# Issuing the load of xs from ScalarE's queue, behind that of xg, in the second stage of a graph-GRU kernel

## The chip, the cores and the metric

The kernel runs on one core of one Trainium2 chip. The metric is the device time of one launch in microseconds. Three runs of the kernel before gave 2310.07, 2310.32 and 2313.84 us; their median is 2310.32 us.

## The reference

For each of 2048 samples x is a matrix of 50 nodes by 32 features. Two maskers (T = 2) make an adjacency matrix each out of the sample, a gated cell mixes neighbours with it, and then come a batch norm, a layer norm and an attention pooling:

```python
adj = relu(einsum('bn,tnm->btm', x.reshape(b, 1600), masker_param) + masker_bias).reshape(b, 2, 50, 50)
adj = adj / (adj.sum(-1, keepdims=True) + 1e-6)
h = broadcast(x, (b, 2, 50, 32))
m = einsum('btnm,btmd->btnd', adj, h @ weight)
r, z, ng = split(m @ w_ih.T + b_ih + h @ w_hh.T + b_hh, 3)
h = (1 - sigmoid(z)) * tanh(sigmoid(r) * ng) + sigmoid(z) * h
# batch norm over b, layer norm over (t, n, d), softmax of scores over n, weighted sum over n
```

## The kernel before

All three stages run on one core, one after the other. Samples come in 16 tiles of 128.

**Stage 1** (up to about 1466 us of the profile) computes the adjacency in split float32 products and stores it, transposed, in the DRAM tensor `adjT`. **Stage 2** (about 1468 to 2080 us) is the gated cell. **Stage 3** does the norms and the pooling. The change touches stage 2 alone.

In stage 2 a tile is worked off in 8 rounds (`ROUNDS`), called q = 0 to 7 here; two tiles, r = 0 and 1, make one iteration of a hardware loop (16 steps, s = 8r + q; iterations 1 to 6 are the loop, 0 and 7 stand outside of it). The buffers `adj_sb`, `xs_sb` and `xg_sb` are double, one half for each r. `xs` holds x by node, padded with zeros (tensor `xz`), and `xg` holds the same x by feature.

- **TensorE** (`turn`, line 720): in step s it first aggregates the next step, `aggregate(s + 1)` (matmuls of `xs` and `adj`, line 674, into a PSUM bank), then does `gates(s)`: the matmuls of the r and z gates (line 699), four transposes of an earlier tile's result (`turn_chunks`, line 716), and the matmuls of the n gate (line 705). `gates` waits for `m_ready`, the low half of the aggregate, which VectorE writes (line 570). At s = 6 and 14 it waits until `adj_loaded[r]` has counted the three transfers of a tile: two halves of the adjacency and `xs`, 16 each, so 48 (lines 682 to 685).
- **ScalarE** (`turn`, line 507), in order: `m_hi` of the next step (line 490), in four of the eight rounds a part of `xg_hi` (line 486), the sigmoid of r in two halves (line 520), the sigmoid of z in two halves (line 525, after `h_ready` of the step before), the copy of four transposes to `hC` (line 498), the tanh (line 530, after `n_in`), the store of that `hC` (line 505), and at q = 0 of a tile the load of `xg` for the next tile (line 477).
- **VectorE** (`turn`, line 616), in order: `m_lo` of the next step (line 570), `n_in` (line 580), the statistics of `hC` (line 603, after `hC_ready`), the three operations that end the cell (lines 590, 593 and 595, after the tanh), and in four of the eight rounds a transpose of `hG` into `hT` (line 614).
- **SyncE** only loads: once `ax_done` says that tile t has been aggregated it issues the three transfers of tile t + 2 into the buffers that are free by this, in the order adjacency half 0, adjacency half 1, `xs`.

An adjacency half is moved in runs of 256 bytes (64 float32), 5000 of them; `xs` is moved in 100 rows of 16 KB.

Of the kernel before, what the change touches and what calls it, by code (L numbers as in the profile page):

```python
# [58 lines left out]
ROUNDS = 32 // QB  # L59
# [18 lines left out]
def wait(eng, sem, value):  # L78

    if not (isinstance(value, int) and value <= 0):  # L80
        eng.wait_ge(sem, value)
# [297 lines left out]
def stage2(nc, psum, ins, adjT, hF, stats):  # L379


    with ExitStack() as ctx:
# [3 lines left out]
        xs = sb("xs_sb", [2 * N, 2, SH, 2 * D])  # L386
# [23 lines left out]
        adj_loaded = [sem("adj_loaded0"), sem("adj_loaded1")]  # L410
        xg_loaded = [sem("xg_loaded0"), sem("xg_loaded1")]
        xg_hi_ready, xg_ready = sem("xg_hi_ready"), sem("xg_ready")
        ax_done, m_hi_ready, m_ready = sem("ax_done"), sem("m_hi_ready"), sem("m_ready")
# [11 lines left out]
        def rz_bank(pair):  # L425

            return psum[:, (2 + pair) * BANK:(2 + pair) * BANK + RC]
# [8 lines left out]
        @block.sync  # L436
        def _(sp):
            def load_adj(tile, r):
                for half in range(2):
                    sp.dma_start(adj[N * half:N * half + N, r], adjT[tile, :, SH * half:SH * half + SH].rearrange("(c m) s -> m c s", m=N)  # L440
                                 ).then_inc(adj_loaded[r], 16)
                sp.dma_start(xs[:, r], ins["xz"][tile]).then_inc(adj_loaded[r], 16)

            def load_xg(tile, r):
                sp.dma_start(xg[:, r], ins["xg"][tile]).then_inc(xg_loaded[r], 16)

            def iteration(it, more):
                for r in range(2):
                    tile = it * 2 + r
                    if more:  # L450
                        sp.wait_ge(ax_done, (tile + 1) * ROUNDS)
                        load_adj(tile + 2, r)

            for dst, src in ((wT4, "wT4"), (wih, "wihT"), (whh4, "whhT4"), (biases, "biases")):
                sp.dma_start(dst[:], ins[src]).then_inc(consts_loaded, 16)
            load_xg(0, 0)
            load_adj(0, 0)
            sp.dma_start(ident[:], ins["ident"]).then_inc(ident_loaded, 16)
            load_xg(1, 1)
            load_adj(1, 1)  # L460
            iteration(0, True)
            with sp.Fori(1, TILES // 2 - 1) as it:
                iteration(it, True)
            iteration(TILES // 2 - 1, False)
            for n in range(len(batches)):
                sp.wait_ge(hC_stored[n], 16 * TILES)

        @block.scalar
        def _(act):
            act.wait_ge(blocks_ready, 1)  # L470
            nc.scalar.copy(wd_hi[:], wd[:]).then_inc(wd_hi_ready, 1)
            act.wait_ge(bias_ready, 1)

            def load_xg(tile, r):

                act.wait_ge(h_ready, (tile - 1) * ROUNDS)
                nc.scalar.dma_start(xg[:, r], ins["xg"][tile]).then_inc(xg_loaded[r], 16)

            def x_hi(it, r, k):

                if k == 0:
                    act.wait_ge(xg_loaded[r], (it + 1) * 16)

                    wait(act, gates_done, it * S if r else it * S - ROUNDS)
                g = slice(k * XG, (k + 1) * XG)
                nc.scalar.copy(xg_hi[:, r, g], xg[:, r, g]).then_inc(xg_hi_ready, 1)  # L486

            def m_halves(it, s):
                act.wait_ge(ax_done, it * S + s + 1)
                nc.scalar.copy(m_hi[:, s % 2], ax_bank(s)).then_inc(m_hi_ready, 1)  # L490

            def evacuate(tile, n):

                act.wait_ge(turned, tile * len(batches) + n + 1)
                wait(act, hC_stored[n], 16 * tile)
                wait(act, bn_done, (tile - 1) * len(batches) + n + 1)
                c0, c1 = batches[n]
                nc.scalar.copy(hC[:, c0:c1, :].rearrange("p c b -> p (c b)"),  # L498
                               turn_bank[:, 0:(c1 - c0) * P]).then_inc(hC_ready, 1)

            def store(tile, n):

                act.wait_ge(hC_ready, tile * len(batches) + n + 1)
                c0, c1 = batches[n]
                nc.scalar.dma_start(hF[tile, :, c0:c1, :], hC[:, c0:c1, :]).then_inc(hC_stored[n], 16)

            def turn(it, more):
                for s in range(S):
                    r, q = divmod(s, ROUNDS)
                    if s + 1 < S or more:  # L510
                        wait(act, gates_done, it * S + s)
                        m_halves(it + (s + 1) // S, (s + 1) % S)
                    k = s % ROUNDS - (ROUNDS - XPARTS)
                    if 0 <= k < XPARTS and (s < ROUNDS or more):
                        x_hi(it + s // ROUNDS, 1 - s // ROUNDS, k)
                    act.wait_ge(rz_done, it * S + s + 1)
                    wait(act, n_in_ready, it * S + s)
                    for pair in range(2):
                        half = slice(SH * pair, SH * pair + SH)
                        last = nc.scalar.activation(r_gate[half], rz_bank(pair)[half], ACT.Sigmoid, bias=bias[half, R_G:R_G + 1])  # L520
                    last.then_inc(r_ready, 1)
                    wait(act, h_ready, it * S + s)
                    for pair in range(2):
                        half, other = slice(SH * pair, SH * pair + SH), slice(SH - SH * pair, 2 * SH - SH * pair)
                        last = nc.scalar.activation(z_bank[half], rz_bank(pair)[other], ACT.Sigmoid, bias=bias[other, Z_G:Z_G + 1])  # L525
                    last.then_inc(z_ready, 1)
                    if q and (r or not (isinstance(it, int) and it == 0)):
                        evacuate(it * 2 + r - 1, q - 1)
                    act.wait_ge(n_in_ready, it * S + s + 1)
                    nc.scalar.activation(n_bank(s), n_in[:, s % 2], ACT.Tanh).then_inc(n_ready, 1)  # L530
                    if q and (r or not (isinstance(it, int) and it == 0)):
                        store(it * 2 + r - 1, q - 1)
                    if q == 0 and (r and more or not r and not (isinstance(it, int) and it == 0)):
                        load_xg(it * 2 + r + 1, 1 - r)

            for k in range(XPARTS):
                x_hi(0, 0, k)
            m_halves(0, 0)
            turn(0, True)
            with act.Fori(1, TILES // 2 - 1) as it:  # L540
                turn(it, True)
            turn(TILES // 2 - 1, False)
            for n in range(len(batches)):
                evacuate(TILES - 1, n)
                store(TILES - 1, n)
# [810 lines left out]
```

## Time and profile before

| | us |
|---|---|
| median of three runs | 2310.32 (2310.07 to 2313.84) |
| the profiled execution's own time | 2318.24 |
| its span, first to last instruction | 2316.5 |
| ScalarE busy over the span | 962.2 (42%) |
| VectorE busy over the span | 1091.0 (47%) |
| TensorE busy over the span | 2198.9 (95%) |

Shares over the span mix three stages. Between 1700 and 1900 us, inside stage 2, TensorE is busy 199.98 of 200 us, VectorE 172.58 and ScalarE 177.36. The end of a matmul is modelled in the profile, so TensorE's share says that it has work queued, and the idle time before its weight loads (the engine name PEld) tells more about its waits. The queues from which transfers are issued are named SPq (SyncE) and ACTq (ScalarE); the time of a row there is that of the issue, not of the transfer.

### The profile page before, as it was taken

The numbers are of one execution on the slowest core, as the hardware profiler recorded it, in microseconds if no ns is written. First come the engines' busy times: TensorE is split into PE (matmuls) and PEld (weight loads), VectorE is DVE, ScalarE is ACT, GpSimd is POOL, SyncE is SP. The second block draws the span as 40 slices with busy tenths as digits, with TensorE's granted clock in tenths as the row PEclk, the third lists the DMA queues.
The fourth block names the chain that finished last, engine by engine and source line by source line (L and its number), as shares of the span: only waits on it lengthen the run. The fifth ranks groups of instructions, "written<-read, shape, count | busy, mean of one in ns | idle before, by whom it ended". The sixth has DMA issues, their size and how long they took to land. (4 is left out here: it accounts for less than half of the span.)

```text
span 2316.5 us, 34741 instructions
## 1 busy us (share of the span) xinstructions
PE 2198.9 (95%) x12302; PEld 1737.8 (75%) x12302; DVE 1091.0 (47%) x2177; ACT 962.2 (42%) x1637; POOL 136.2 (6%) x124
## 2 busy tenths in 40 slices
PE   8999999999999999999999999299999999975888
PEld 7888888888888888888888888277777777752333
DVE  4433233332345223333233332178888888873656
ACT  4322122221234212222122221088888988865551
POOL 0000000000000000000000000011101111104340
PEclk9999999999999999999999999699999999986899
DMA  6421222212234222221222211577777677619440
GB/s 208 151 75 44 88 91 90 74 45 88 92 128 143 64 90 90 91 69 50 89 90 91 72 48 27 124 171 184 186 201 181 188 199 181 181 65 261 122 119 5
DMA packets 341744, 264.06 MB, mean 114 GB/s; under 512 B 169334, under 2 KB 302998, under 8 KB 339990
## 3 DMA queue, kind: packets, MB, share of 16 engines
q1 hardware_dynamic: 323546, 225.69, 34.5%
q10 hardware_dynamic: 18144, 37.69, 5.0%
q8 instruction: 29, 0.48, 0.1%
q14 instruction: 25, 0.20, 0.0%
HBM read 195.65 MB, written 67.70 MB: 114 GB/s over the span
## 5 line engine op out<-in xcount | busy, mean ns | idle before, releaser
L340 PE MATMUL psum<-w_hi,x_lo 128*128 128x500 f32 x2080 | 823.0, 396 | 8.6 <-DVE w_lo L216 8.6
L340 PE MATMUL psum<-w_lo,x_hi 128*128 128x500 f32 (+1 forms) x2080 | 811.0, 390 | 0.0
L340 PE MATMUL psum<-w_hi,x_hi 128*128 128x500 f32 x1920 | 745.1, 388 | 0.0
L276 DVE TENSOR_REDUCE rows<-u 128x10 f32<-128x500 f32 x160 | 107.7, 673 | 893.5 <-ACT u L229 892.8
L340 PEld LDWEIGHTS psum<-w_hi,x_lo 128*128 128x128 f32 x2080 | 392.1, 188 | 84.4 <-issue 7.9
L340 PEld LDWEIGHTS psum<-w_lo,x_hi 128*128 128x128 f32 (+1 forms) x2080 | 392.5, 189 | 73.2
L340 PEld LDWEIGHTS psum<-w_hi,x_hi 128*128 128x128 f32 x1920 | 361.7, 188 | 72.9
L235 ACT COPY at<-psum 125x512 f32<-125x512 f32 x160 | 93.8, 586 | 677.4 <-PE psum L321 677.4
L229 ACT ACTIVATE u<-psum 128x500 f32<-128x500 f32 x160 | 94.1, 588 | 342.4 <-PE psum L340 342.3
L674 PE MATMUL psum<-adj_sb,xs_sb 100*64 100x100 f32 x2048 | 200.6, 350 | 30.1 <-DMA xs_sb<-xz 30.1
L674 PEld LDWEIGHTS psum<-adj_sb,xs_sb 100*64 100x64 f32 x2048 | 144.4, 149 | 73.9 <-issue 63.7
L652 POOL TENSOR_TENSOR xg_lo<-xg_sb,xg_hi 128x400 fp32r<-128x400 f32 x64 | 67.1, 1049 | 1961.4 <-ACT xg_hi L486 1961.4
L520 ACT ACTIVATE r_gate<-psum,bias 64x400 f32<-64x400 f32 x256 | 151.2, 591 | 18.3 <-PE psum L699 15.8
L216 DVE TENSOR_TENSOR w_lo<-w_raw,w_hi 128x1000 fp32r<-128x1000 f32 x120 | 144.1, 1201 | 23.6 <-ACT w_hi L210 17.4
L210 ACT CAST w_hi<-w_raw 128x1000 fp32r<-128x1000 f32 (+1 forms) x140 | 135.6, 969 | 46.3 <-PE psum L340 45.0
L525 ACT ACTIVATE psum<-psum,bias 64x400 f32<-64x400 f32 x256 | 142.3, 556 | 12.7 <-DVE hG L595 6.9
L284 DVE TENSOR_TENSOR an<-u,rows 128x500 f32<-128x500 f32 x160 | 108.8, 680 | 6.9
L603 DVE BATCH_NORM_STATS2 stats<-hC 128x128 f32 (+1 forms) x400 | 88.7, 282 | 49.3 <-ACT hC L498 48.9
L321 PEld LDWEIGHTS psum<-ident_sb,an 128*125 128x125 f32 x640 | 94.1, 186 | 17.8 <-DVE an L284 3.2
L321 PE MATMUL psum<-ident_sb,an 128*125 128x128 f32 x640 | 96.0, 272 | 4.0 <-DVE an L284 4.0
L1013 DVE SCALAR_TENSOR_TENSOR pr<-h,nmu_sb,psum 128x512 f32<-128x512 f32 x100 | 70.5, 743 | 47.0 <-PE psum L1221 24.6
L570 DVE TENSOR_TENSOR m_lo<-psum,m_hi 128x400 fp32r<-128x400 f32 x128 | 70.6, 552 | 28.6 <-ACT m_hi L490 28.6
(160 smaller groups left out, 2284.8 us busy)
## 6 DMA issues: line engine op xcount, KB each, us to landing
w_raw<-W SPq DMA_DIRECT2D x140, 500.0 KB, 7.9
adjT<-at SPq DMA_DIRECT2D x160, 250.0 KB
adj_sb<-adjT SPq DMA_DIRECT2D x32, 1250.0 KB
xs_sb<-xz SPq DMA_DIRECT2D x16, 1600.0 KB
hF<-hC ACTq DMA_DIRECT2D x96, 256.0 KB, 6.7
h<-hF SPq DMA_DIRECT2D x64, 256.0 KB, 4.5
xg_sb<-xg ACTq DMA_DIRECT2D x14, 800.0 KB, 8.0
h<-hF SPq DMA_DIRECT2D x48, 192.0 KB, 3.7
```

The source lines that it names most:

```text
L210: nc.scalar.copy(w_hi[:, k0:k1, :], w_raw[:, k0:k1, :]).then_inc(w_hi_ready, 1)
L216: nc.vector.tensor_tensor(w_lo[:, k0:k1, :], w_raw[:, k0:k1, :], w_hi[:, k0:k1, :].bitcast(fp32), ALU.subtract).then_inc(w_ready, 1)
L229: nc.scalar.activation(u[:, c2].rearrange("p n m -> p (n m)"), mm_out(c2), ACT.Relu).then_inc(u_ready, 1)
L235: nc.scalar.copy(at[:, c2].rearrange("p k b -> p (k b)"), tr_out(c2)).then_inc(at_ready, 1)
L276: nc.vector.tensor_reduce(rows[:, 0], u[:, c2], AX.X, ALU.add).then_inc(dve_step, 1)
L284: nc.vector.tensor_tensor(an[:, c2], u[:, c2], rows[:, 2].unsqueeze(2).to_broadcast([P, GN, N]), ALU.mult).then_inc(an_ready, 1)
L321: last = nc.tensor.transpose(tr_out(c2)[:, k * P:(k + 1) * P], flat[:, k * RK:(k + 1) * RK], ident[:, :])
L340: last = nc.tensor.matmul(mm_out(w % 2), a[0:r, k, cols], b[0:r, k, :], start=k == 0 and n == 0, stop=k == KF and n == 1)
L520: last = nc.scalar.activation(r_gate[half], rz_bank(pair)[half], ACT.Sigmoid, bias=bias[half, R_G:R_G + 1])
L525: last = nc.scalar.activation(z_bank[half], rz_bank(pair)[other], ACT.Sigmoid, bias=bias[other, Z_G:Z_G + 1])
L603: last = nc.vector.bn_stats(stats[:, bass.ds(tile, 1), c, :].rearrange("p i v -> p (i v)"), hC[:, c, :])
L674: last = nc.tensor.matmul(out_[SH * i:SH * i + SH, :, gi], xs[:, r, b, :], adj[:, r, :, b], start=True, stop=True)
```

## The change

The load of `xs` leaves `load_adj` and becomes a function `load_xs`. For the first two tiles SyncE still issues it, right behind the adjacency. For tiles 2 to 15 ScalarE issues it, behind the load of `xg` for the same tile, at q = 0 of the tile before, after a wait for `ax_done` of the tile that used the buffer last. The semaphore and its count of 48 stay.

```diff
--- before.py
+++ after.py
@@ -439,6 +439,8 @@
                 for half in range(2):
                     sp.dma_start(adj[N * half:N * half + N, r], adjT[tile, :, SH * half:SH * half + SH].rearrange("(c m) s -> m c s", m=N)
                                  ).then_inc(adj_loaded[r], 16)
+
+            def load_xs(tile, r):
                 sp.dma_start(xs[:, r], ins["xz"][tile]).then_inc(adj_loaded[r], 16)
 
             def load_xg(tile, r):
@@ -455,9 +457,11 @@
                 sp.dma_start(dst[:], ins[src]).then_inc(consts_loaded, 16)
             load_xg(0, 0)
             load_adj(0, 0)
+            load_xs(0, 0)
             sp.dma_start(ident[:], ins["ident"]).then_inc(ident_loaded, 16)
             load_xg(1, 1)
             load_adj(1, 1)
+            load_xs(1, 1)
             iteration(0, True)
             with sp.Fori(1, TILES // 2 - 1) as it:
                 iteration(it, True)
@@ -475,6 +479,11 @@
 
                 act.wait_ge(h_ready, (tile - 1) * ROUNDS)
                 nc.scalar.dma_start(xg[:, r], ins["xg"][tile]).then_inc(xg_loaded[r], 16)
+
+            def load_xs(tile, r):
+
+                act.wait_ge(ax_done, (tile - 1) * ROUNDS)
+                nc.scalar.dma_start(xs[:, r], ins["xz"][tile]).then_inc(adj_loaded[r], 16)
 
             def x_hi(it, r, k):
 
@@ -532,6 +541,7 @@
                         store(it * 2 + r - 1, q - 1)
                     if q == 0 and (r and more or not r and not (isinstance(it, int) and it == 0)):
                         load_xg(it * 2 + r + 1, 1 - r)
+                        load_xs(it * 2 + r + 1, 1 - r)
 
             for k in range(XPARTS):
                 x_hi(0, 0, k)
```

## Rows read from the trace of the kernel before

**Rows 1.** Waits, 1531 to 2030 us: who waited for whom; total, times, longest.

```profile
PEld psum L674 <- issue: 30.2, 114, 0.3
PEld psum L699 <- DVE m_lo L570: 13.2, 43, 0.4
```

**Rows 2.** Timeline of SyncE's queue, one tile: start us, us taken, operation.

```profile
1741.55 8.48 SPq L440 DMA_DIRECT2D adj_sb<-adjT  x2
1750.20 8.66 SPq L442 DMA_DIRECT2D xs_sb<-xz  x1
1776.65 8.50 SPq L440 DMA_DIRECT2D adj_sb<-adjT  x2
```

**Rows 3.** Windows at that tile's end: busy us by engine, clock, DMA share, GB/s.

```profile
1773.50:1775.50 2.00, 2.00 (x18) 1.70 (x18) 1.93 (x5) 1.87 (x5) 1.05 (x1) 1.00 0.16 60
1775.50:1777.50 2.00, 2.00 (x24) 1.56 (x20) 1.12 (x6) 1.87 (x4) 0.00 (x0) 1.00 0.00 0
```

**Rows 4.** Line 477, load of xg: its issues in ns, its landing in us.

```profile
L477 ACTq DMA_DIRECT2D xg_sb<-xg x14: 357/361/393, 1543.5 to 2000.3; - x14
DMA to landing us min/median/max: 7.6/8.0/8.3
```

**Rows 5.** Timeline of ScalarE, from its issue of that load, same tile.

```profile
1754.56 0.51 ACT L530 ACTIVATE psum<-n_in 128x400 f32<-128x400 f32 x1 [1.01 <-DVE n_in L580]
1754.79 0.36 ACTq L477 DMA_DIRECT2D xg_sb<-xg  x1
1755.27 0.49 ACT L490 CAST m_hi<-psum 128x400 fp32r<-128x400 f32 x1 [0.19 <-issue]
1755.65 1.20 ACT L520 ACTIVATE r_gate<-psum,bias 64x400 f32<-64x400 f32 x2
1756.92 1.13 ACT L525 ACTIVATE psum<-psum,bias 64x400 f32<-64x400 f32 x2
1758.08 0.59 ACT L498 COPY hC<-psum 128x512 f32<-128x512 f32 x1
```

**Rows 6.** Timeline of VectorE beside it.

```profile
1753.46 0.54 DVE L570 TENSOR_TENSOR m_lo<-psum,m_hi 128x400 fp32r<-128x400 f32 x1
1757.73 0.54 DVE L570 TENSOR_TENSOR m_lo<-psum,m_hi 128x400 fp32r<-128x400 f32 x1
1758.19 0.62 DVE L580 SCALAR_TENSOR_TENSOR n_in<-psum,bias,r_gate 128x400 f32<-128x400 f32 x1
1758.81 0.87 DVE L603 BATCH_NORM_STATS2 stats<-hC 128x128 f32 x4
1762.20 0.53 DVE L570 TENSOR_TENSOR m_lo<-psum,m_hi 128x400 fp32r<-128x400 f32 x1
```

**Rows 7.** Timelines of ScalarE and VectorE, a step where VectorE waits for hC.

```profile
1771.48 0.59 ACT L498 COPY hC<-psum 128x512 f32<-128x512 f32 x1
...
1772.20 0.87 DVE L603 BATCH_NORM_STATS2 stats<-hC 128x128 f32 x4 [0.88 <-ACT hC L498]
```

**Rows 8.** Timeline of TensorE's weight loads, beside rows 5 and 6.

```profile
1754.04 0.19 PEld L699 LDWEIGHTS psum<-m_hi,wd_lo 64*128 64x128 f32 x2 [0.35 <-DVE m_lo L570]
1758.52 0.19 PEld L699 LDWEIGHTS psum<-m_hi,wd_lo 64*128 64x128 f32 x2 [0.29 <-DVE m_lo L570]
1762.98 0.19 PEld L699 LDWEIGHTS psum<-m_hi,wd_lo 64*128 64x128 f32 x2 [0.29 <-DVE m_lo L570]
```

**Rows 9.** ScalarE at tile 1, the first that issues a load of xg.

```profile
1544.99 1.19 ACT L520 ACTIVATE r_gate<-psum,bias 64x400 f32<-64x400 f32 x2 [0.49 <-PE psum L699]
1546.09 1.12 ACT L525 ACTIVATE psum<-psum,bias 64x400 f32<-64x400 f32 x2
```

**Rows 10.** ScalarE at tile 14, the last that issues one.

```profile
2002.69 0.56 ACT L525 ACTIVATE psum<-psum,bias 64x400 f32<-64x400 f32 x1 [0.24 <-DVE hG L595]
```

**Rows 11.** Lines 132 and 126, stage 1's loads: issue durations, ns min/median/max.

```profile
L132 SPq DMA_DIRECT2D w_raw<-W x140: 332/430/1187, 1.2 to 1327.0; - x140
L126 SPq DMA_DIRECT2D x_raw<-xT x32: 327/367/3509, 0.8 to 740.3; - x32
```

## The prediction

> **What bounds the kernel now.** I read the waits of stage 2 first, then the timeline of SyncE's queue over one tile, the DMA share at the end of that tile, and last the timelines of the three compute engines where ScalarE issues the load of xg. The waits decide the outline: from 1531 to 2030 us no engine waits for a transfer. TensorE's idle time before its weight loads comes in small pieces, 30.2 / 114 = 0.26 us where it is put down to issue and 13.2 / 43 = 0.31 us where it is put down to m_lo [rows 1], so in this stage it goes from one group of matmuls to the next. The reader is to see in the queue's timeline that a tile takes 1776.65 - 1741.55 = 35.10 us, and that SyncE is through with its issues at 1750.20 + 8.66 = 1758.86 and then has nothing to do until 1776.65 [rows 2]. In the windows all transfers of the tile have ended before 1775.5, since the DMA share is 0.16 and then 0.00 [rows 3]; TensorE asks for them just before 1776.65, when the aggregation that lets SyncE go is done. So the loads are on time by 1.1 us or more, with xs the last of them.
>
> **What the change can give back: nothing on the path.** SyncE's issue of xs, 8.66 us behind the adjacency [rows 2], goes away 14 times, but behind it stands only SyncE's own wait of 17.8 us. No engine waits for xs, so an earlier landing shortens nothing either. This edit is costed at 0; its cover is SyncE's idle time, and were it gone nothing would get longer, as the issue is gone too.
>
> **The transfer itself.** xs now starts later: issued at about 1755.3 instead of 1750.2, behind xg, which lands 8.0 us after its issue [rows 4], so at 1762.8. Before, xs stood behind the adjacency, whose 10,000 short runs let SyncE finish its issue of xs only at 1758.86 [rows 2]. The bytes of the tile are the same and the engines are kept busy by the rest of the adjacency while xg passes, so I take the same end, before 1775.5, and the same cover of 1.1 us. If the landing slips past it, TensorE waits the difference (a rival below). The stores of hC behind it in ScalarE's queue land later, by at most the time to the end of the tile's traffic (1775.5 - 1758.9 = 17 us for the first of them); each is needed when its part of hC is overwritten one tile later, 35.1 us on, so they stay hidden. The load of xg stays ahead of xs and keeps its landing.
>
> The Trainium skill, DMA: Bandwidth & Descriptors, section Issuing engines are not separate DMA queues, says that transfers started by different engines run on the same 16 DMA engines, and that another issuer saves only the issue time. By that rule the gain would be SyncE's 8.66 us, and the trace shows that nobody waits for those: 0 by the rule and by the rows. It speaks against the change, because the issue is now paid by an engine with work behind it.
>
> **The issue on ScalarE: the term that counts.** At q = 0 ScalarE's tanh starts at 1754.56, the issue of xg at 1754.79 and ends 1755.15, and m_hi starts at 1755.27 [rows 5]. A second issue costs its own 0.36 us (357 to 393 ns over all 14 of that line [rows 4]) and the register work and the wait ahead of it, 1754.79 - 1754.56 = 0.23 us, together 0.59 us. The wait for ax_done is for an event more than ten microseconds old and costs no more. The trace has no issue of xs with nothing long ahead of it; I take xg's price, as it has 128 rows and xs has 100. Behind the issue on ScalarE stand, in order, m_hi, the sigmoids of r and z, the copy to hC and the tanh of q = 1. How far does it get?
>
> - ScalarE: the sigmoid of r starts 0.59 later. From r to z the shortest distance is 1546.09 - 1544.99 = 1.10 us [rows 9]; here it is 1756.92 - 1755.65 = 1.27 [rows 5], so 0.17 us of slack takes its part. z and the copy to hC come 0.59 - 0.17 = 0.42 us later. (If the 0.07 us between the end of r at 1756.85 and z were all the slack, it would be 0.52.)
> - VectorE: the statistics start at 1758.81, which is both the end of n_in, 1758.19 + 0.62 [rows 6], and the end of the copy to hC, 1758.67 [rows 5], with 0.13 us on top. That 0.13 is a latency and no slack: in a step where VectorE was idle for hC it also started 1772.20 - (1771.48 + 0.59) = 0.13 us after the copy's end [rows 7]. From there to m_lo at 1762.20 VectorE goes without a gap, and from m_lo to m_lo it takes 4.47 us, which is TensorE's own pace. So m_lo is 0.42 us late.
> - TensorE: at 1754.04 it started 0.04 us after m_lo's end (1753.46 + 0.54 = 1754.00) [rows 6, 8], so it can. At 1758.52 and 1762.98 it started 0.25 us after m_lo's end, with an idle time of 0.29 us, nearly the 0.26 us that it spends where no engine is named [rows 1, 8]. So 0.21 us of the lateness is swallowed and 0.42 - 0.21 = 0.21 us is left. After that TensorE has no idle time to win it back, so it stays in the tile.
>
> **The sum.** Of the 14 issues 12 stand in the loop and look like this one: 12 x 0.21 = 2.5 us. At tile 1 ScalarE idles 0.49 us for TensorE right after [rows 9], and at tile 14 0.24 us before z [rows 10], where outside of the loop the register work falls away too; both cost 0 to 0.2, I take 0. Against the profiled execution's own 2318.24 us (span 2316.5) this is 2320.8; profiled time lies 7.9 us above the median of the runs, a difference that the change has no part in, so the forecast is 2310.3 + 2.5 = 2312.8 us, longer by 0.11%.
>
> **Bounds of the unknown.** Below: if the 0.13 us before the statistics is slack after all, 0.29 us reaches VectorE and 0.08 TensorE, 12 x 0.08 = 1 us; if nothing reaches it, 0. Above: the loads of stage 1, issued behind one another, take 430 ns at the median and up to 1187 ns, those of x 3509 ns [rows 11]. At 1.19 us the issue is 0.83 longer than xg's, and all of the excess arrives: 12 x (0.21 + 0.83) = 12.5, and 0.6 more each at tiles 1 and 14, so 13.7 us and 2324.0. The nearest row is xg's own, from the same queue and moment.
>
> **Rivals.**
>
> 1. Wholly hidden: what ScalarE loses is taken up before TensorE sees it. For it: ScalarE idles up to 1.01 us before the tanh of q = 0. Against it: that idle time lies ahead of the issue. Time 2310.3 to 2311.3.
> 2. No slack at TensorE (slower): the 0.29 us is a fixed price that is paid after the wait ends. All of the 0.42 to 0.52 us arrives, 12 times: 5.0 to 6.2 us, 2315.3 to 2316.6. For it: m_lo is named as what ended these waits in 43 cases [rows 1]. Against it: the start 0.04 us after m_lo at 1754.04. It decides from 0.39 us per tile.
> 3. A dearer issue (slower): xs behind xg, or beside SyncE's long adjacency, blocks ScalarE for 0.7 to 1.2 us. 12 x (0.34 to 0.83) on top of 2.5: 6.6 to 12.5 us, 2317 to 2323. For it: the longer issues of stage 1 [rows 11], and 8.66 us for this same transfer [rows 2]. Against it: xg is issued at 0.36 us with the adjacency under way. If it blocked for 8.66 us as on SyncE, it would be 12 x 8.5 = 102 us, 2412; for that the queue ahead would have to hold thousands of runs, and it holds 128.
> 4. The load comes late (slower): xs, started later, ends after 1776.65. The tile's traffic would have to take 1.1 us more of some 34 before TensorE waits; each microsecond over that costs 14 us, and 1 to 2 of them give 2324 to 2338. For it: xs starts with 20 us to go (1755.3 to 1775.5) and has the rest of the adjacency beside it, where it had the queue to itself. Against it: the DMA engines have 1.1 us of idle time and the same bytes.
> 5. Faster: the executions without the profiler may hide a wait for xs that this one does not have, and an earlier landing would remove it. At 0.4 us a tile, 14 tiles: 5.6 us, 2304.7. No row speaks for it; it is left for what a trace can't show.
>
> **How the numbers follow.** What a measurement of this kernel can tell from no change is about 0.2%, 4.6 us. Chances: forecast 0.36, rival 1 0.20, rival 2 0.15, rival 3 0.17, rival 4 0.05, rival 5 0.07. The forecast and rival 1 lie within 4.6 us: same 0.56. Rivals 2 to 4: slower 0.37. Rival 5: faster 0.07. The predicted time is 2312.8. The range leaves out rivals 4 and 5 and the dear end of rival 3: 2309.6 to 2320.5.
>
> **What would show it.** The period of SyncE's waits should be 35.3 us instead of 35.10; the issue of xs on ScalarE 0.36 us; m_hi at q = 0 0.6 us later against the tanh, the z sigmoid, the statistics and the m_lo of two steps on 0.4 us later; the idle time before TensorE's weight loads of line 699 at q = 2 0.5 us and no longer 0.29; still no wait for a DMA. An issue above 0.6 us, idle time of 0.7 us at q = 2, or a wait of TensorE for xs or the adjacency would make the prediction wrong.

## The result, and the profile after

With the change the kernel takes 2318.13 us (median of 11 runs, 2315.18 to 2321.37); the kernel before, run beside it, 2313.84 us (11 runs, 2310.07 to 2317.34). The medians lie 4.3 us apart. The ratio is 1.002, with a 95% interval of 1.0011 to 1.0029, which is 2.5 to 6.7 us: slower, but by about as little as the prediction counted as no change (0.2%, 4.6 us). The forecast was 2312.8 us and 2.5 us longer, its range 2309.6 to 2320.5. The time lies in the range, 5.3 us above the forecast. Of these 3.5 us are the level of the kernel before, whose median was 2310.32 in the three runs that the forecast started from and is 2313.84 in eleven; 1.8 us are the change.

The profiled execution alone would not have shown it: its own time is 2318.93 us against 2318.24, its span 2317.2 us against 2316.5. Stage 2, from SyncE's first issue of the adjacency to its first issue for stage 3, took 2086.69 - 1471.71 = 614.98 us against 611.73, which is 3.25 us more. The first two tiles, whose loads are issued as before, took 0.5 us less of it than in the other profile; from SyncE's issue for the third tile on (1531.59 us, before 1531.46) it is 555.10 us against 551.38, 3.72 us more. Stage 3, which the change doesn't touch, took 230.5 against 233.6. Over all ten profiles of this case stage 3 lies between 227.6 and 234.8 us in no order with the edits, so below I compare stage 2, and in it the length of a tile.

The timeline of SyncE's queue after, at the same two tiles as [rows 2]. The issue of xs is gone from it, and the tile takes 35.40 us:

```profile
1743.05 8.64 SPq L440 DMA_DIRECT2D adj_sb<-adjT  x2
...
1778.45 8.64 SPq L440 DMA_DIRECT2D adj_sb<-adjT  x2
```

Over the last eleven tiles, from the issue at 1601.36 to that at 1990.98, it is 389.62 / 11 = 35.42 us, against (1987.31 - 1601.23) / 11 = 35.10 before.

The timeline of ScalarE after, at q = 0 and into q = 1, which answers to [rows 5]. Look at m_hi: it starts 1757.43 - 1756.23 = 1.20 us behind the tanh, where it was 0.71, and its idle time is put down to issue:

```profile
1756.23 0.51 ACT L539 ACTIVATE psum<-n_in 128x400 f32<-128x400 f32 x1 [1.01 <-DVE n_in L590]
1756.45 0.36 ACTq L481 DMA_DIRECT2D xg_sb<-xg  x1
1756.98 0.34 ACTq L486 DMA_DIRECT2D xs_sb<-xz  x1
1757.43 0.49 ACT L499 CAST m_hi<-psum 128x400 fp32r<-128x400 f32 x1 [0.70 <-issue]
1757.82 1.19 ACT L529 ACTIVATE r_gate<-psum,bias 64x400 f32<-64x400 f32 x2
1758.92 1.11 ACT L534 ACTIVATE psum<-psum,bias 64x400 f32<-64x400 f32 x2
1760.06 0.59 ACT L507 COPY hC<-psum 128x512 f32<-128x512 f32 x1
```

So the second issue costs ScalarE 0.49 us by the first reading, and 0.70 - 0.19 = 0.51 us by the idle time. From r to z it is now 1.10 us, the shortest distance there is, where it was 1.27: 0.17 us are taken up there. Next VectorE, which answers to [rows 6]; its statistics now wait 0.32 us for the copy to hC, and from m_lo to m_lo it is 4.79 us instead of 4.47:

```profile
1759.40 0.53 DVE L580 TENSOR_TENSOR m_lo<-psum,m_hi 128x400 fp32r<-128x400 f32 x1
1759.86 0.61 DVE L590 SCALAR_TENSOR_TENSOR n_in<-psum,bias,r_gate 128x400 f32<-128x400 f32 x1
1760.79 0.88 DVE L613 BATCH_NORM_STATS2 stats<-hC 128x128 f32 x4 [0.32 <-ACT hC L507]
...
1764.19 0.53 DVE L580 TENSOR_TENSOR m_lo<-psum,m_hi 128x400 fp32r<-128x400 f32 x1
```

Last TensorE's weight loads, which answer to [rows 8]. The first row is a step that [rows 8] don't have, the gates of q = 0, where the idle time was 0.29 us in the kernel before:

```profile
1751.54 0.22 PEld L709 LDWEIGHTS psum<-m_hi,wd_lo 64*128 64x128 f32 x2 [0.44 <-issue]
...
1755.71 0.19 PEld L709 LDWEIGHTS psum<-m_hi,wd_lo 64*128 64x128 f32 x2 [0.38 <-DVE m_lo L580]
...
1760.19 0.19 PEld L709 LDWEIGHTS psum<-m_hi,wd_lo 64*128 64x128 f32 x2 [0.29 <-DVE m_lo L580]
...
1764.78 0.19 PEld L709 LDWEIGHTS psum<-m_hi,wd_lo 64*128 64x128 f32 x2 [0.42 <-DVE m_lo L580]
```

The rows are the gates of q = 0, 1, 2 and 3 (the prediction and the expectations call the last one q = 2). TensorE loses time at three of them: 0.44 - 0.29 = 0.15 us at q = 0, 0.38 - 0.35 = 0.03 at q = 1, nothing at q = 2, and 0.42 - 0.29 = 0.13 at q = 3, together 0.31 us of the 0.32 by which the tile is longer. From q = 3 to q = 7 TensorE's gates follow each other as before. Rows of the waits between 1531 and 2030 us, which answer to [rows 1] (us in total, times, longest):

```profile
PEld psum L709 <- issue: 21.0, 65, 0.6
...
PEld psum L709 <- DVE m_lo L580: 16.0, 48, 0.4
ACT m_hi L499 <- issue: 11.8, 20, 0.7
```

No engine waits for a transfer here either. The windows at the end of the tile, as [rows 3]; the DMA share is 0.00 from 1777 on, and SyncE issues the next at 1778.45:

```profile
1775.00:1777.00 2.00, 2.00 (x16) 1.74 (x16) 1.93 (x5) 1.88 (x5) 1.06 (x1) 1.00 0.38 144
1777.00:1779.00 2.00, 2.00 (x24) 1.62 (x22) 1.12 (x4) 1.94 (x4) 0.00 (x0) 1.00 0.00 0
```

### The profile page after: what moved, and what is told of

Same layout as the page of the kernel before. It is cut to its first block and busy times, and to the rows that moved or that the text cites. A ratio compares the mean times of both kernels' runs of the same rounds, so it can differ in the third digit from the quotient of the medians.

```text
span 2317.2 us, 34741 instructions
## 1 busy us (share of the span) xinstructions
PE 2201.2 (95%) x12302; PEld 1738.7 (75%) x12302; DVE 1088.9 (47%) x2177; ACT 958.1 (41%) x1637; POOL 136.4 (6%) x124
```

## The experiments

The lengths of stage 2 and of a tile in it come from the timelines of SyncE's queue, as above (the tile: mean over the last eleven). Where the number of runs is 1, the time is that of the profiled execution alone; with stage 3 moving by up to 7 us it says little, and the reading rests on the tile.

| kernel | tile, us | stage 2, us | time, us (runs) | what it does |
|---|---|---|---|---|
| before | 35.10 | 611.7 | 2313.84 (11) | |
| the change | 35.42 | 615.0 | 2318.13 (11) | |
| e1 | 35.41 | 614.7 | 2320.09 (1) | before, and an idle second issue at q = 0 |
| e2 | 35.10 | 611.9 | 2313.50 (1) | xs from GpSimd's queue |
| e3 | 35.10 | 611.4 | 2313.95 (11) | the change, xg issued ahead of the tanh |
| e4 | 35.90 | 620.7 | 2323.95 (1) | the change, and a third issue |
| e5 | 35.03 | 610.2 | 2312.51 (1) | before, half the statistics |
| e6 | 35.03 | 610.0 | 2309.54 (1) | the change, half the statistics |
| e7 | 35.27 | 614.0 | 2317.58 (1) | the change, xs issued at q = 2 |
| e8 | 35.11 | 611.7 | 2312.57 (12) | the change, xs issued at q = 1 |

**e1, an idle issue.** In the kernel before:

```diff
                         load_xg(it * 2 + r + 1, 1 - r)
+                        wait(act, marked, 16 * (it * 2 + r - 1))
+                        nc.scalar.dma_start(mark_out, biases[:, 0, :]).then_inc(marked, 16)
```

> Theory (the issue costs, not the transfer): what makes a tile longer is that ScalarE is held for a second issue behind the tanh of q = 0. This kernel is the one before, with xs still issued by SyncE behind the adjacency, and with an idle transfer of 12 bytes a row out of the biases issued by ScalarE behind that of xg at q = 0, 14 times. The tile should take 35.4 us as with the change (35.10 before), m_hi at q = 0 should stand idle 0.7 us for issue, the adjacency should keep the DMA engines to itself. Rival (the transfer costs: xs beside the adjacency or in front of the stores of hC slows something): the tile stays at 35.1 us, since no large transfer was moved.

The tile took 35.41 us, as with the change, though all large transfers stood where they were. ScalarE at q = 0:

```profile
1754.63 0.36 ACTq L479 DMA_DIRECT2D xg_sb<-xg  x1
1755.10 0.38 ACTq L538 DMA_DIRECT2D mark_out<-biases_sb  x1
1755.59 0.49 ACT L492 CAST m_hi<-psum 128x400 fp32r<-128x400 f32 x1 [0.68 <-issue]
```

The reader sees the same picture with 12 bytes a row as with 16 KB: the issue takes 0.38 us and ScalarE stands idle for 0.68 us before m_hi. The price is that of an issue, with 12 bytes a row as with 16 KB. The rival falls.

**e2, the same transfer from elsewhere.** In the change, ScalarE's call goes, and GpSimd issues ahead of its work for that tile:

```diff
+                pool.wait_ge(ax_done, (tile - 1) * ROUNDS)
+                pool.wait_ge(n_ready, (tile - 1) * ROUNDS + 1)
+                nc.gpsimd.dma_start(xs[:, r], ins["xz"][tile]).then_inc(xs_loaded[r], 16)
...
+                    pe.wait_ge(xs_loaded[0], it * 16 + 16)
```

> The load of xs for tiles 2 to 15 goes out at the same moment as with the change (after the tanh of q = 0), but from GpSimd's queue, so it runs beside the adjacency and ScalarE has no second issue. Theory (the issue costs): the tile takes 35.10 to 35.15 us, m_hi at q = 0 idle 0.2 us. Rival (the transfer costs): 35.4 us. It can't part them if GpSimd's transfers come so late that TensorE waits for xs; then a wait for a DMA shows at line 700 and its length is taken off.

35.10 us, and no wait of TensorE for a transfer. m_hi at q = 0 again:

```profile
1753.69 0.49 ACT L495 CAST m_hi<-psum 128x400 fp32r<-128x400 f32 x1 [0.19 <-issue]
```

With e1 this parts the two halves of the change: the issue without the transfer costs all, the transfer without the issue nothing. Here the transfer comes from a third queue; e3 has it in ScalarE's own.

**e3, the issue of xg into idle time.**

```diff
+                    if q == 0 and (r and more or not r and not (isinstance(it, int) and it == 0)):
+                        load_xg(it * 2 + r + 1, 1 - r)
                     act.wait_ge(n_in_ready, it * S + s + 1)
                     nc.scalar.activation(n_bank(s), n_in[:, s % 2], ACT.Tanh).then_inc(n_ready, 1)
...
-                        load_xg(it * 2 + r + 1, 1 - r)
                         load_xs(it * 2 + r + 1, 1 - r)
```

> The change, with the load of xg issued ahead of ScalarE's wait for n_in at q = 0, where ScalarE idles 1.01 us, and that of xs behind the tanh, where that of xg stood. Theory (the issue costs only where it stands in the way): 0.6 us of issue goes into idle time, the tile takes 35.10 us and the time is that of the kernel before, ratio 1.000 (within 0.001), against 1.002 with the change as it is. Rival (the transfer costs): still 35.4 us and 1.002. Second rival (two issues cost what they cost on ScalarE wherever they stand): 35.4 us.

The tile took 35.10 us; 2313.95 us (11 runs) against 2314.37 of the kernel before beside it, ratio 0.9997 (0.9988 to 1.0006). ScalarE:

```profile
1751.76 0.36 ACTq L481 DMA_DIRECT2D xg_sb<-xg  x1
...
1753.67 0.51 ACT L541 ACTIVATE psum<-n_in 128x400 f32<-128x400 f32 x1 [1.01 <-DVE n_in L591]
1753.81 0.34 ACTq L486 DMA_DIRECT2D xs_sb<-xz  x1
1754.27 0.49 ACT L499 CAST m_hi<-psum 128x400 fp32r<-128x400 f32 x1
```

The issue of xg at 1751.76 now runs while ScalarE still has sigmoids to do, the tanh starts after 1.01 us of idle time as before, and m_hi follows it by 0.60 us. Both issues are there, xs moves from ScalarE's queue as with the change, and the loss is gone, so both rivals fall.

**e4, a third issue.**

```diff
                         load_xs(it * 2 + r + 1, 1 - r)
+                        wait(act, marked, 16 * (it * 2 + r - 1))
+                        nc.scalar.dma_start(mark_out, biases[:, 0, :]).then_inc(marked, 16)
```

> The change, and a third issue (12 bytes a row) behind xs at q = 0. Theory (two loops without slack): the first extra issue lost 0.51 us on ScalarE, of which 0.2 us was slack between the sigmoids of r and z, and 0.32 us arrived in the tile. The slack is used up, so the third issue arrives whole: the tile takes 35.4 + 0.5 = 35.9 us, 7 us over the stage more than with the change. Rival (TensorE or VectorE win it back in the second half of the tile): less than 0.2 us more, up to 35.6 us.

35.90 us, 0.48 us more than with the change: the third issue arrives whole, where 0.32 of 0.51 arrived of the second. Two rows of the waits, 1600 to 2030 us:

```profile
ACT m_hi L501 <- issue: 15.8, 18, 1.1
...
PE psum L713 <- ACT psum L536: 4.3, 12, 0.4
```

The second of them names what the profile of the change left at "issue": at the gates of q = 0 TensorE waits for ScalarE's sigmoid of z (here line 536), 12 times, once for each tile of the loop.

**e5 and e6, half the statistics.** In the kernel before and in the change (the statistics, and with them the result, are of 64 samples of 128):

```diff
-                                              hC[:, c, :])
+                                              hC[:, c, 0:SH])
```

> The kernel before with the batch statistics of stage 2 taken over 64 of a chunk's 128 samples (the result is then another one): VectorE's line 603 gets shorter by about a quarter of a microsecond in each round. It is the pair of the next kernel. Both theories: TensorE sets the pace, the tile takes 35.0 to 35.1 us, at most 0.08 less for the m_lo that came late at q = 0.

> The change with the same shorter statistics. Theory (the delay is carried by the ring sigmoid of z, copy to hC, statistics, the cell's last three operations, next sigmoid of z, which takes 4.46 us against TensorE's 4.46 to 4.48 a round and so can't catch up): with 0.25 us taken out of each lap ScalarE and VectorE catch up within one or two rounds, TensorE's wait at q = 0 for the sigmoid of z goes, that for m_lo at q = 2 shrinks, and the tile takes as long as the pair's, within 0.05 us. Rival (the delay is an additive price of the issue, however much slack the ring has): 0.32 us more than the pair's.

Both took 35.03 us a tile, and each of the last eleven tiles did. Rows of e6: the statistics in rounds q = 1 and q = 2, and two of its waits between 1600 and 2030 us:

```profile
1756.89 0.61 DVE L613 BATCH_NORM_STATS2 stats<-hC 128x64 f32 x4 [0.32 <-ACT hC L507]
...
1761.09 0.60 DVE L613 BATCH_NORM_STATS2 stats<-hC 128x64 f32 x4
```

```profile
ACT m_hi L499 <- issue: 10.5, 18, 0.7
...
PEld psum L709 <- DVE m_lo L580: 0.9, 3, 0.3
```

ScalarE's m_hi is held up as in the change (0.7 us at its longest), and the statistics at q = 1 still wait 0.32 us for the copy. One round later nothing waits, and TensorE waits for m_lo 3 times for 0.9 us in all, where with the change it is 46 times for 15.4 us over the same stretch. So the issue has no price of its own; it costs what VectorE and ScalarE can't catch up.

**e7, the issue at q = 2.**

```diff
                         load_xg(it * 2 + r + 1, 1 - r)
-                        load_xs(it * 2 + r + 1, 1 - r)
+                    if q == 2 and (r and more or not r and not (isinstance(it, int) and it == 0)):
+                        load_xs(it * 2 + r + 1, 1 - r)
```

> The change with the load of xs issued at the end of q = 2 (behind the store of hC) instead of q = 0, two rounds or 9 us later. Theory: m_hi is held 0.5 us there too, but between the sigmoids of r and z at q = 3 there are 0.38 us of slack instead of 0.17 to 0.2, since ScalarE waits for hG, so 0.13 us are left for the ring, less than TensorE's slack of 0.19 us: the tile takes 35.1 to 35.2 us. The adjacency has the DMA engines to itself and lands near 21 us again; xs starts at 24 us and lands at 33 to 34, still ahead of 35.1. Rival (each issue on ScalarE costs 0.3 us wherever it is placed): 35.4 us. If xs comes late, TensorE waits for a DMA at s = 6 and 14, and the tile is longer by that wait, which the waits will name.

The mean is 35.27 us, and the tiles are of two kinds: some of 35.0 and some of 35.4 to 35.6. ScalarE around the issue, and two rows of the waits, 1600 to 2030 us:

```profile
1763.34 0.34 ACTq L486 DMA_DIRECT2D xs_sb<-xz  x1
1763.79 0.49 ACT L499 CAST m_hi<-psum 128x400 fp32r<-128x400 f32 x1 [0.67 <-issue]
1764.18 1.19 ACT L529 ACTIVATE r_gate<-psum,bias 64x400 f32<-64x400 f32 x2
1765.28 1.11 ACT L534 ACTIVATE psum<-psum,bias 64x400 f32<-64x400 f32 x2
```

```profile
ACT m_hi L499 <- issue: 12.1, 29, 0.9
...
PE psum L710 <- DMA xs_sb<-xz: 2.1, 6, 0.5
```

m_hi is held up 0.67 us as elsewhere, and five of the eleven tiles are none the longer for it. But xs comes too late in half of the tiles: TensorE waits for it 6 times by name, up to 0.5 us. The expectation that it would still be in time was wrong. Two effects are mixed here, since a wait of TensorE for xs also lets the other two engines catch up, so this run alone doesn't show what the issue costs at q = 2; e8 takes the waits away.

**e8, the issue at q = 1.** As e7 with `q == 1`.

> The change with the load of xs issued at the end of q = 1, behind the store of hC: one round earlier than in the run before, so that xs has 4.5 us more to land, and one round later than with the change. Theory: at q = 2 there are 0.36 us of slack between the sigmoids of r and z, of an issue of 0.51 us 0.15 are left for the ring, less than TensorE's slack of 0.19: the tile takes 35.03 to 35.10 us, no wait of TensorE for a DMA, and the time is that of the kernel before (ratio 0.999 to 1.0005). Rival (the price of the issue is the same wherever it is placed, and the 35.03 us of the undisturbed tiles at q = 2 came from waits for xs that let the ring catch up): 35.4 us, ratio 1.002.

The tile took 35.11 us; 2312.57 us (12 runs) against 2313.72 beside it, ratio 0.9992 (0.9984 to 1.0001). ScalarE behind the issue, first in the kernel before and then in e8, and a row of e8's waits, 1600 to 2030 us:

```profile
1759.93 1.20 ACT L520 ACTIVATE r_gate<-psum,bias 64x400 f32<-64x400 f32 x2
1761.39 1.13 ACT L525 ACTIVATE psum<-psum,bias 64x400 f32<-64x400 f32 x2 [0.27 <-DVE hG L595]
```

```profile
1757.78 0.49 ACT L499 CAST m_hi<-psum 128x400 fp32r<-128x400 f32 x1 [0.59 <-issue]
1758.17 1.19 ACT L529 ACTIVATE r_gate<-psum,bias 64x400 f32<-64x400 f32 x2
1759.27 1.11 ACT L534 ACTIVATE psum<-psum,bias 64x400 f32<-64x400 f32 x2
```

```profile
PEld psum L710 <- DVE m_lo L581: 13.3, 43, 0.4
```

From r to z it is 1761.39 - 1759.93 = 1.46 us in the kernel before, and 1.10 here: 0.36 us of the issue is taken up where ScalarE waited for VectorE's hG. There is no wait for a transfer, and the m_lo waits are those of the kernel before (13.3 us, 43 times, against 15.4 us, 46 times, with the change over the same stretch). So the place of an issue decides on its price. The half of the rival that explained the 35.03 us of e7 by the waits for xs fits: without them it is 35.11.

## Why the prediction was right, and where not

- **What bounds stage 2, and what the change gives back.** Right: TensorE's pace, no wait for a transfer before or after. SyncE's wait for the aggregation (line 674, after the change 684) grew from 231.0 to 353.4 us over 14 tiles, which is 8.7 us each, the issue time that it was relieved of; nobody used it. The rule that the prediction took from the Trainium skill (DMA: Bandwidth & Descriptors, section Issuing engines are not separate DMA queues), that another issuer saves issue time alone, held. What it leaves to the reader is that the new issuer pays, as e1 shows.
- **The issue on ScalarE, 0.59 us.** 0.49 to 0.51 measured. From the end of the first issue to the start of the second it is 1756.98 - (1756.45 + 0.36) = 0.17 us, where 0.23 was taken from the distance between the tanh and the first. The issue itself took 0.34 us (0.36 said), at tile 1 0.60.
- **Slack between the sigmoids, 0.17 us.** Measured 0.17, and the 0.13 us before the statistics was a latency, as said: they wait for the copy now, 0.32 us. So 0.32 reach VectorE, not 0.42, by the dearer issue that was assumed.
- **TensorE, 0.21 us a tile.** This is the step that failed in part. At q = 3, where m_lo is late, it loses 0.13 us: 0.32 less the slack of 0.19 to 0.21. But the prediction looked no further than m_lo and took the part that TensorE's slack swallows for gone. It isn't: ScalarE and VectorE are still that much behind, and 0.15 us more are lost five rounds later, at the gates of q = 0, to the sigmoid of z, and 0.03 at those of q = 1. The sum of 2.5 us should have been 12 x 0.32 = 3.8 us; the runs have 3.72 from the third tile on in the profile and 4.3 (2.5 to 6.7) in the timed ones. That 2.5 is no further off is in part luck, as two errors work against each other: with the issue at its measured 0.49 us the prediction's own working gives 12 x (0.32 - 0.21) = 1.3 us.
- **Why it comes back five rounds later.** The prediction looked at VectorE's own round in stage 2, 4.47 us from m_lo to m_lo, as long as TensorE's of 4.46 to 4.48 us. A second ring, no shorter, was missed: it goes from ScalarE's sigmoid of z over the copy to hC and VectorE's statistics and cell to the next sigmoid of z. A lap of it after the change, on ScalarE and on VectorE:

```profile
1763.38 1.13 ACT L534 ACTIVATE psum<-psum,bias 64x400 f32<-64x400 f32 x2 [0.52 <-DVE hG L605]
1764.53 0.58 ACT L507 COPY hC<-psum 128x512 f32<-128x512 f32 x1
...
1767.84 1.13 ACT L534 ACTIVATE psum<-psum,bias 64x400 f32<-64x400 f32 x2 [0.36 <-DVE hG L605]
```

```profile
1765.25 0.87 DVE L613 BATCH_NORM_STATS2 stats<-hC 128x128 f32 x4
1766.04 0.55 DVE L600 TENSOR_TENSOR n_in<-xg_sb,psum 128x400 f32<-128x400 f32 x1
1766.63 0.57 DVE L603 TENSOR_TENSOR n_in<-n_in,psum 128x400 f32<-128x400 f32 x1
1767.23 0.57 DVE L605 TENSOR_TENSOR hG<-n_in,psum 128x400 f32<-128x400 f32 x1
```

From 1763.38 to 1767.84 it is 4.46 us, and each step starts within 0.14 us of the end of the one before it in the ring; nothing outside the ring is waited for: z ends at 1764.51, the copy at 1765.11, the statistics start 0.14 us later, and the last operation of the cell ends at 1767.80. What it is late at q = 1 it is late at q = 6, until at q = 7 only one transpose is copied and one chunk counted. Just there TensorE meets it at the gates of q = 0. e6 shows it from the other side: with statistics of 0.60 us in place of 0.87 the rings catch up, and the whole 0.32 us is gone.
- **Tiles 1 and 14, and the rivals.** Tile 1 cost nothing (from SyncE's issue at 1531.59 us to the next it is 34.58 us, as before), and the stretch from the last of these issues to stage 3, with tile 14's, is 95.71 us against 95.53; both were taken as 0 out of 0 to 0.2. Rival 1 (wholly hidden) is out, since TensorE loses time at three gates. Rival 2 (no slack at TensorE) was the nearest by what it adds, 5.0 to 6.2 us against 4.3, with a wrong mechanism: all that reaches VectorE does arrive in the tile, but the slack is there, since TensorE loses 0.13 us of 0.32 at q = 3, and the rest comes back by the ring. Rival 3 (a dearer issue) is out but for tile 1. Rival 4 (a late load) did not occur with the change; it did in e7, where xs was issued two rounds later. Rival 5 (faster) is out, as the interval of the ratio lies above 1.
- **The end of the transfers.** Right in sum, and wrong on the way: it isn't xs that ends later but the adjacency beside it, as the last section shows. The forecast of what would show it was right in kind; the period was given as 35.3 and is 35.42, the idle time at q = 3 (called q = 2) as 0.5 and is 0.42.

What stays open is why stage 3 differs by up to 7 us from profile to profile.

## What to carry to other kernels

An issue is work of the engine that issues it, about half a microsecond here, and its price is set by the place: free in front of a wait that the engine has anyway (e3) and nearly so where a later sigmoid has 0.36 us to spare (e8), dear where every ring that passes the engine is as long as the round of the bounding engine. A delay on a ring without slack is not over where it is first swallowed; follow it until the ring has a short lap, and look for every meeting with the bound engine on the way. Moving a load off a queue that idles half of the time gave nothing here, though its issue took 8.66 us there.

## What the runs showed of the hardware

The transfers of two queues share the engines in a way that I had not expected. While xs moves in 16 KB rows from ScalarE's queue (q10), the adjacency in its 256-byte runs on SyncE's (q1) nearly stands still. Eight microseconds of the kernel before (1763 to 1771), with xs alone on q1 (packets, MB, share of 16 engines):

```profile
q1 hardware_dynamic: 85, 1.36, 53.6%
q10 hardware_dynamic: 198, 0.36, 14.4%
```

and eight microseconds of the kernel after (1764.5 to 1772.5), in which q1 still has adjacency to move:

```profile
q10 hardware_dynamic: 237, 1.62, 65.7%
q1 hardware_dynamic: 131, 0.03, 2.2%
```

In these eight microseconds q1 moved 131 packets; in the two from 1755 to 1757, with xs not yet moving, it had moved 1279. The 1.62 MB of q10 are for the most part rows of xs of 16 KB, 82 of its 237 packets. Between 1764 and 1772 the trace has 83 rows of xs and 94 packets of q1, and 78 of the 83 rows start within 12 ns of the end of a packet of q1, as if each engine took one of each in turn, however large. In e3, with xs again in ScalarE's queue, it is 78 and 78 between 1760 and 1768; in e2, with xs in GpSimd's, 71 rows and 49 packets of q1 between 1760 and 1766, so there it isn't one for one. The Trainium skill, DMA: Bandwidth & Descriptors, section Queues, rings and completion order, says that an engine goes round its queues by packets, of several descriptors each; the trace agrees as far as the turns go, and here a turn looks like a single packet as the profile counts them. This is read off the packets and was not tested by a run of its own. So the adjacency, which in the kernel before had all but ended when xs began to move, still moves 213 packets on q1 between 1772 and 1776, with the next tile's issue at 1778.45. The total ends in time all the same: in this tile nothing moves any more from 1777 on, 1.4 us before that issue.
